# First attention of a token tower: half of the weighted values as fp16 products

## The reference

```python
def _L1_attn_ref(v, WQ, WK, WV, Wout, bout):
    q = (v @ WQ).reshape(B, S, H, C)
    k = (v @ WK).reshape(B, S, H, C)
    val = (v @ WV).reshape(B, S, H, C)
    scores = jnp.einsum('bshc,bthc->bsth', q, k) * SCALE
    A = jax.nn.softmax(scores, axis=2)
    u = jnp.einsum('bsth,bthc->bshc', A, val).reshape(B, S, H * C)
    return u @ Wout + bout
h = h + _L1_attn_ref(_layernorm(h, axis=-1), ...)
```

## Time and profile before

| what | us |
|---|---|
| time, median of 3 runs | 4917.94 (4913.84 to 4918.95) |
| the profiled execution | 4918.01 |
| its span | 4916.3 |
| first exponential of the first attention | 715.0 |
| last exponential of the first attention | 2837.2 |
| GpSimd, q to fp16 (L1473), mean of one | 0.610 |
| GpSimd, low part of q (L1475) | 1.159 |
| GpSimd, multiplication of the add (L1481) | 1.042 |
| GpSimd, addition into h (L1484) | 1.267 |
| VectorE, one row maximum (L1716) | 0.685 |
| ScalarE, one exponential (L1561) | 1.110 |

### The profile page before, as it was taken

How to read it: one execution, slowest core, us unless ns; L and a number is a source line. 1 busy time by engine, 2 the same in 40 slices (tenths; PEclk the granted TensorE clock), 3 DMA queues, 4 the chain that set the end, 5 groups by cost and what they waited for, 6 DMA issues and landing times. The chain is left out here.

```text
span 4916.3 us, 106442 instructions
## 1 busy us (share of the span) xinstructions
PE 4586.0 (93%) x42579; PEld 2033.3 (41%) x42579; DVE 3655.1 (74%) x6356; ACT 3150.1 (64%) x3450; POOL 2325.2 (47%) x2279
## 2 busy tenths in 40 slices
PE   5999969999999999999999979999999999999965
PEld 3433423333333333333333334444444444444433
DVE  4677756666666666666666678888888888888878
ACT  2444426666666666666666638888888888888844
POOL 3455553333333323233333346666666666666656
PEclk9999979999999999999999979999999999999966
DMA  4212100000000000000000000000000000000001
GB/s 102 69 52 69 35 1 1 1 1 1 1 1 1 1 1 1 1 1 1 1 1 1 1 1 2 2 2 2 2 2 2 2 2 2 2 3 2 2 7 28
DMA packets 43624, 51.44 MB, mean 10 GB/s; under 512 B 33416, under 2 KB 33544, under 8 KB 43144
## 3 DMA queue, kind: packets, MB, share of 16 engines
q1 hardware_dynamic: 40440, 44.03, 3.4%
q10 hardware_dynamic: 2704, 0.72, 0.1%
HBM read 39.73 MB, written 4.19 MB: 9 GB/s over the span
## 5 line engine op out<-in xcount | busy, mean ns | idle before, releaser
L1716 DVE TENSOR_REDUCE a_mp<-psum 128x1 f32<-128x512 f32 x2072 | 1324.8, 685 | 667.8 <-PE psum L1593 654.1
L2442 DVE TENSOR_REDUCE f_mp<-psum 128x1 f32<-128x512 f32 (+2 forms) x2352 | 1472.7, 684 | 187.1 <-PE psum L2264 171.0
L1561 ACT ACTIVATE a_prob<-psum,escale 128x1024 f32<-128x1024 f32 x1024 | 1086.3, 1110 | 524.6 <-PE psum L1642 524.6
L2224 ACT ACTIVATE f_prob<-psum,escale_f 128x1024 f32<-128x1024 f32 x1152 | 1247.2, 1112 | 217.1 <-PE psum L2341 108.4
L1650 PE MATMUL psum<-a_prob,a_v 128*64 128x512 f32 x4104 | 994.2, 605 | 0.0
L2078 POOL TENSOR_SCALAR f_hi<-f_raw,part 128x512 f16<-128x512 f32 x324 | 506.2, 1562 | 393.8 <-ACT f_raw L2182 387.5
L2264 PE MATMUL psum<-f_kf,f_qf 64*128 64x512 f16 (+2 forms) x3658 | 652.6, 307 | 40.1 <-DVE f_mp L2442 31.2
L1481 POOL TENSOR_TENSOR a_u<-a_og,a_inv 128x512 f32<-128x512 f32 x129 | 134.4, 1042 | 1167.4 <-DVE a_inv L1731 1167.4
L2354 PE MATMUL psum<-f_prob,f_vh 128*32 128x512 f32 (+3 forms) x6144 | 614.7, 495 | 9.3 <-DVE f_oc L2464 7.3
L2333 PE MATMUL psum<-f_qf,f_kf 64*128 64x512 f16 (+3 forms) x3074 | 505.5, 327 | 18.9 <-ACT f_og L2187 18.2
L1650 PEld LDWEIGHTS psum<-a_prob,a_v 128*64 128x64 f32 x4104 | 249.0, 136 | 505.1 <-issue 501.5
(11 more groups left out here) (448 smaller groups left out, 6942.4 us busy)
## 6 DMA issues: line engine op xcount, KB each, us to landing
idx<-in_itok_BS_dram SPq DMA_DIRECT2D x36, 512.0 KB, 6.0
idx<-in_itok_BS_dram SPq DMA_DIRECT2D x54, 256.0 KB, 6.9
idx<-in_x_dram SPq DMA_DIRECT2D x18, 256.0 KB, 3.6
a_qh<-a_rowT SPq DMA_DIRECT2D x258, 1.0 KB
out_dram<-h SPq DMA_DIRECT2D x16, 256.0 KB, 2.6
f_qf<-f_rowT SPq DMA_DIRECT2D x130, 4.0 KB, 1.7
wd<-in_L_ffn_Wd_dram SPq DMA_DIRECT2D x2, 256.0 KB
bd<-in_L_ffn_bd_dram ACTq DMA_DIRECT2D x16, 2.0 KB
```

The costliest lines, as they stand in the source:

```text
L1561: act.activation(prob[:, part], k.psum[:, pair:pair + 2].rearrange("p b n -> p (b n)"), ACT.Exp, scale=k.escale[:]).then_inc(s.read, 1)
L1716: dve.tensor_reduce(mp[:, tg % 2, t + 4 * r, c:c + 1], bank_of(j + r), X, ALU.max)\
L2224: act.activation(prob[:, u % NPF], k.psum[:, pair:pair + 2], ACT.Exp, scale=k.escale_f[:])\
L2442: dve.tensor_reduce(side[:, at[0]:at[-1] + 1:step], bank_of(j + r)[:, 0:len(at) * width].rearrange("p (a b) -> p a b", b=width), X, ALU.ma ...
```

## The change

Key tiles 0, 1, 4 and 5 of each head no longer go into the value sum as f32. Their exponentials are held as a high fp16 part (`ph`) and a low one (`pl`), the values too (`vh`, `vl`), and TensorE adds three fp16 products instead of one f32 product. Tiles 2, 3, 6 and 7 stay f32.

- The parts of tiles 0 and 4 are both made by GpSimd (`halve`). For tiles 1 and 5 ScalarE makes the high part (a copy behind the exponential of tile 2 or 6) and VectorE the low one (`low`).
- `A_PARTS` puts the f32 parts first: (2,3), (0,1), (6,7), (4,5), in slots 4, 6, and 1 and 2 of the next round, so the fp16 parts are used four to five steps after their exponentials.
- The copy of a head's sum moves from behind exponential 1 to behind exponential 3, and "out" from behind the third item to behind the fourth.
- GpSimd's order is written anew; its add for a head comes one round later. `twice` splits the values once per batch.
- The exponentials get a bias of 6 ln 2, a factor of 64 that the division takes out again.
- Four new tiles are cleared at the start; four semaphores of an earlier stage are used again.

```diff
-A_PARTS = ((0, 1), (2, 3), (4, 5), (6, 7))
+A_PARTS = ((2, 3), (0, 1), (6, 7), (4, 5))
+A_PART_OF = {kt: p for p, part in enumerate(A_PARTS) for kt in part}
+A_HALVED = {0: 0, 1: 1, 4: 2, 5: 3}
+A_LEVEL = 6 * math.log(2.0)
-A_VALUES_AT = (2, 4, 6, 9)
+A_VALUES_AT = (4, 6, 9, 10)
-A_EXTRA = {0: (('x', 0),), 1: (('q', 2),), 3: (('out', -1),)}
-A_COPY_AT = 1
+A_EXTRA = {0: (('x', 0),), 1: (('q', 2),), 4: (('out', -1),)}
+A_COPY_AT = 3
...
+                def twice(b, par, n):
+                    here = v[:, par, :, 0]
+                    pool.tensor_copy(vh[:, par], here).then_inc(s.p, 1)
+                    passed(pool, k.seen, s.p, n + 5)
+                    pool.tensor_tensor(vl[:, par], here, vh[:, par], ALU.subtract).then_inc(s.p, 1)
+
+                def halve(G, kt, count):
+                    at = A_HALVED[kt]
+                    passed(pool, k.seen, s.read, count)
+                    pool.tensor_copy(ph[:, at], prob[:, kt]).then_inc(s.p_high, 1)
+                    passed(pool, k.seen, s.p_high, n_half(G, kt))
+                    pool.tensor_tensor(pl[:, at], prob[:, kt], ph[:, at], ALU.subtract).then_inc(s.p_low, 1)
...
+                pool.memset(ph[:], 0.0).then_inc(s.clear, 1)
+                pool.memset(pl[:], 0.0).then_inc(s.clear, 1)
+                pool.memset(vh[:, 1], 0.0).then_inc(s.clear, 1)
+                pool.memset(vl[:, 1], 0.0).then_inc(s.clear, 1)
+                pool.memset(level[:], A_LEVEL).then_inc(s.clear, 1)
...
+                        split_q(G + 2, (x + 2) % 4, n_stream(i, x, "q", 0))
+                        halve(G, 0, n_stream(i, x, "exp", 0))
+                        if G > 1:
+                            add(i * 2 + (x - 2) // HEADS, x % 2, G)
+                        if x % HEADS == 4:
+                            prepare_batch(b, (x // HEADS + 1) % 2, b * 6)
+                        if x % HEADS == 5:
+                            split_x(b, (x // HEADS + 1) % 2, n_stream(i, x, "x", 0))
+                        halve(G, 4, n_stream(i, x, "exp", 4))
                         if x % HEADS == 3:
                             squares(i * 2 + x // HEADS)
+                        if x % HEADS == 6:
+                            twice(b, (x // HEADS + 1) % 2, b * 6)
...
-                            act.wait_ge(s.pv, n_pv(G - 1, part // 2))
+                            act.wait_ge(s.pv, n_pv(G - 1, A_PART_OF[part]))
                             act.activation(prob[:, part], k.psum[:, pair:pair + 2].rearrange("p b n -> p (b n)"),
-                                           ACT.Exp, scale=k.escale[:]).then_inc(s.read, 1)
+                                           ACT.Exp, scale=k.escale[:], bias=level[:]).then_inc(s.read, 1)
+                            if part in (2, 6):
+                                act.wait_ge(s.read, n_stream(i, x, "exp", part - 1))
+                                act.activation(ph[:, A_HALVED[part - 1]], prob[:, part - 1], ACT.Copy).then_inc(s.p_high_act, 1)
                             if part == A_COPY_AT:
                                 copy_out(G)
...
+                    if A_PARTS[p][0] in A_HALVED:
+                        pe.wait_ge(s.p_low, n_half(G, A_PARTS[p][0]))
+                        pe.wait_ge(s.p_low_dve, n_half(G, A_PARTS[p][1]))
+                        for kt in A_PARTS[p]:
+                            at = A_HALVED[kt]
+                            for a, b in ((vl, ph), (vh, pl), (vh, ph)):
+                                for half in range(2):
+                                    last = pe.matmul(ps[A_SUM][halves(half)], lhsT=a[:, bp, kt],
+                                                     rhs=b[:, at, half * HALF:(half + 1) * HALF],
...
+                def low(G, kt):
+                    at = A_HALVED[kt]
+                    dve.wait_ge(s.p_high_act, n_half(G, kt))
+                    dve.tensor_tensor(pl[:, at], prob[:, kt], ph[:, at], ALU.subtract).then_inc(s.p_low_dve, 1)
...
+                            if u == 0 and i + x:
+                                low(i * AROUND + x - 1, 5)
+                            if u == 4:
+                                low(i * AROUND + x, 1)
```

More of the change, by code:

```diff
@@ L1 @@
 from contextlib import ExitStack
+import math
 import numpy as np
@@ L704, in layer0 @@
         E = {name: k.sem("l0_" + name) for name in L_EVENTS}
+        k.spent, k.spent_at = [E[name] for name in ("gT", "eg", "wT", "gturn")], PAIRS_
         def first(pair):
@@ L1345, in attention1 @@
         prob = sb("a1_prob", [P, NPB, S], F32)
+        ph = sb("a1_ph", [P, 4, S], FP16)
+        pl = sb("a1_pl", [P, 4, S], FP16)
+        vh = sb("a1_vh", [P, 2, T, C], FP16)
+        vl = sb("a1_vl", [P, 2, T, C], FP16)
+        level = sb("a1_level", [P, 1], F32)
         un = sb("a1_un", [P, HALF], F32)
@@ L1509, in _ @@
                         G = i * AROUND + x
+                        b = i * 2 + x // HEADS + 1
+                        split_q(G + 2, (x + 2) % 4, n_stream(i, x, "q", 0))
[7 more added lines that the diff above has]
+                        halve(G, 4, n_stream(i, x, "exp", 4))
                         if x % HEADS == 3:
                             squares(i * 2 + x // HEADS)
[L1512 to L1521, removed]
+                        if x % HEADS == 6:
+                            twice(b, (x // HEADS + 1) % 2, b * 6)
+                add(NB - 1, 0, NB * HEADS)
                 add(NB - 1, 1, NB * HEADS + 1)
@@ L1643, in score, with values @@
                     return last
-                def values(x, p):
+                def values(G, x, p):
                     bp = (x // HEADS) % 2
+                    first, final = A_PARTS[0][0], A_PARTS[-1][-1]
+                    if A_PARTS[p][0] in A_HALVED:
[7 more added lines that the diff above has]
+                                                     rhs=b[:, at, half * HALF:(half + 1) * HALF],
+                                                     start=(kt == first and a is vl), stop=(kt == final and a is vh and b is ph),
+                                                     skip_group_check=True)
+                        last.then_inc(s.pv, 1)
+                        return
                     for kt in A_PARTS[p]:
@@ L1651, in values @@
                                              rhs=prob[:, kt, half * HALF:(half + 1) * HALF],
-                                             start=(kt == 0), stop=(kt == T - 1), skip_group_check=True)
+                                             start=(kt == first), stop=(kt == final), skip_group_check=True)
                     last.then_inc(s.pv, 1)
@@ L1684, in _ @@
                                             pe.wait_ge(s.read, n_stream(i, x, "exp", A_PARTS[p][-1]))
-                                            values(x, p)
+                                            values(G, x, p)
                                         if at == u + T:
                                             pe.wait_ge(s.read, n_stream(i, x - 1, "exp", A_PARTS[p][-1]))
-                                            values(x - 1, p)
+                                            values(G - 1, x - 1, p)
                                 else:
@@ L1699, in _ @@
                         pe.wait_ge(s.read, SS + SR * (NB // 2))
-                        values(-1, p)
+                        values(NB * HEADS - 1, -1, p)
                 pe.wait_ge(s.read, SS + SR * (NB // 2))
```

19 lines of the change are left out of this document (14 added, 5 removed).

## The result

The change made the kernel slower: 4998.46 us (median of 4, 4997.95 to 5001.3) against 4918.44 on the same chip, ratio 1.0165, 95% interval 1.0147 to 1.0183. That is 80 us more, where 17 were forecast; the range ended at 4985.

The account below looks back on a forecast made before the run. The prediction took TensorE to bound the kernel's first attention stretch; 4918.0 - 6 (rounds) + 13 (port) + 7.9 (start) + 1.4 (end) = 4934, stated as 4935 us, slower, range 4895 to 4985.

Parts of the forecast that it names:

- what TensorE saves: Two values parts a round as fp16, 1.39 to 1.40 against 1.87 us each; 1.05 a round with the fifth-slot wait.
- 0.86 + 1.11 + 0.06: Score of tile 7 needs exponential 5's banks, 2.03 us after tile 5's score starts; against 1.68 of work, TensorE waits 0.35.
- 1.01 + 0.95 + 1.01: ScalarE's exponential 2, copy and exponential 3 before the sums' copy, which ends at 4.43 us; TensorE waits 0.65 before "out".
- The 0.09 us wait in the fifth slot goes as well: The second row-maximum matmul's 0.09 us wait for VectorE vanishes, since "out" now stands in front of that M.
- fits: VectorE has 10.8 us of work a round and gets 2.44 more from two subtractions, for which there is room.
- The port, 13 us: VectorE and GpSimd hold each other up on a shared SBUF port pair: +13 us, bounds 0 and 18.
- The two exclude each other: At the port either VectorE comes second (0 to 13 us) or GpSimd is late (18 us), not both.
- Rival B: The port costs more: GpSimd's late subtraction delays VectorE's, the round grows 0.3 to 0.5 us, total 4970 to 5000; 11%.
- The start, 7.9: GpSimd clears four more tiles before making the first input, while TensorE stands idle: +7.9 us.
- Rival A: TensorE's saving comes through, with one or both waits on ScalarE gone: 4800 to 4890 us; 14%.
- Rival C: fp16 products are no faster in this shape, the second values part costs 1.87 us as before: 4996 us; 3%.
- The end: One more values part comes after the last exponential: +1.4 us.

Follow-up runs that it names:

- the best order: Changed kernel without bias, tile 1's copy behind exponential 4, third-slot M earlier, f32 part between scores 5 and 7, VectorE clearing, next input before GpSimd's add: 4820.48 us.
- operand: Changed kernel with the bias tile taken off the exponentials: 4980.47 us, ratio 1.0131.
- M's: Changed kernel with the third slot's row-maximum matmul pair M put ahead of the fp16 values part: 4978.06 us, ratio 1.0126.
- port: Changed kernel without VectorE's two subtractions a round, low parts of tiles 1 and 5 left zero: 4983.80 us, ratio 1.0136.

## Why the prediction was wrong

- **Sign, and what TensorE saves:** the sign of the whole was right, that of a plain round was not (16.29 forecast, 16.72 measured, 16.34 before). The price of an fp16 part was right, 1.41 to 1.42 against 1.39 to 1.40, and the best order gets 0.82 a round out of it (16.34 to 15.52), where 1.05 was put if nothing else waits.
- **The step that failed first: "0.86 + 1.11 + 0.06" and "1.01 + 0.95 + 1.01".** All use the exponential of before, 1.11. The diff adds a second 128x1 operand, and the prediction gave it no term at all. It is 0.093, in 1024 exponentials. The rows were there: a copy with no such operand 1.02, an exponential with one 1.11; the step from none to one could have been taken once more. The Trainium skill states it as well (ScalarE: Activation LUTs, "What ACT_TABLE_LOAD costs": each such operand adds about 93 ns), and the trace agrees: 1.110, 1.203. By TensorE's starts, "out" comes 4.73 after the score of tile 2 instead of 4.53 to 4.57, and tile 7 2.13 after tile 5 instead of 2.03: 0.28 of the 0.44 by which the round was missed; in time 18 us.
- **"The 0.09 us wait in the fifth slot goes as well", and VectorE "fits".** VectorE does have the time over a round. But with the f32 part gone from between them, three M's come within 2.2 us (995.38 to 997.57 above), and six reductions, 0.61 from one start to the next, take 3.7. In plain rounds this lay under ScalarE's wait; in head 2's rounds, with the means among them, it was open. The prediction gave head 2 no term; it was 20 us, with the stretches at a low clock told of below.
- **No term for starting again.** After a wait "out" takes 0.91 to the next start, not 0.84, and the M behind it 0.34, not 0.31; the f32 part to the end is as before, so 0.10 from "out" to the score of tile 5. With 0.02 to 0.03 for the fp16 parts this nearly closes the plain round: 16.29 + 0.28 + 0.10 + 0.03 = 16.70, measured 16.72 to 16.73. What it is worth in time was not run by itself.
- **The port, 13 us:** right in size (15), in part by luck, since 13 was taken between bounds of 0 and 18. About 7 us are in head 4's rounds (0.47 each, where 1.1 was put), 4 in the late head 7's, which the prediction does not name, and the rest in single long rounds. "The two exclude each other" is wrong: in the rows above VectorE comes second, and GpSimd's conversion is then held up as well. Rival B falls, though its 4970 to 5000 takes in the measured time: the plain round does not change without VectorE's subtractions.
- **The start, 7.9:** right. Two clearings on GpSimd, and TensorE's idle, 14.31 against 6.43 in the earlier trace rows:

```profile
679.90 3.52 POOL L1531 MEMSET a_ph<- 128x4096 f16 x1
683.35 3.51 POOL L1532 MEMSET a_pl<- 128x4096 f16 x1
```
```profile
692.58 1.94 PE L1675 MATMUL psum<-ident,a_v 128*128 128x128 f32 x8 [14.31 <-POOL a_v L1477]
```
- **Rival A** falls for this order: the waits are real, and removing the copy's brought 44 us. Rival C falls with the 1.41. The end cost 0.9 (4.35 of idle ahead of the last `un` against 3.46), not 1.4.

The three runs (operand, M's, port; each run's interval is some 8 us to either side) and the start add to 18 + 20 + 15 + 8 = 61 of the 80 us. The rest, some 19, no run took apart, and its cause stays open: by the table, some 8 us of it are in the plain rounds (0.39 more, of which 0.28 is the operand's) and some 8 in head 4's (15, of which 7 went with the subtractions). As waits lie over one another, the shares of single edits need not add up in any case.

## What to carry to other kernels

Price each operand that an edit adds to an instruction on the path, even one that looks free: it was 0.09 us an exponential here. A factor that cancels later might be folded into something that is computed once; no run here did that, and the best kernel leaves it out. A wait taken away shows the next one under it, so before trusting a saving look at what the removed work had kept apart, here the M's and their reductions. And read a group's duration as well as the idle ahead of it: a wait inside a group is in no list of waits.

## What the runs showed that was not expected

In four of the sixteen rounds of head 2, the granted clock of TensorE fell. Timeline of one, VectorE, GpSimd and TensorE:

```profile
1036.55 2.13 POOL L1492 TENSOR_TENSOR a_pl<-a_prob,a_ph 128x1024 f16<-128x1024 f32 x1 [0.47 <-POOL a_ph L1490]
...
1037.65 1.05 DVE L1805 TENSOR_SCALAR mean_f<-mean_f 128x8 f32<-128x8 f32 x1
...
1039.36 0.60 PE L1639 MATMUL psum<-a_xh,a_qh 64*128 64x512 f16 x1 [0.83 <-DVE a_mp L1776]
```

The f32 part behind it took 3.29 instead of 1.94. The stretch from 1039.8 to 1043.1, with the granted clock as the third number from the end:

```profile
1039.80:1043.10 3.30, 3.30 (x9) 0.77 (x8) 3.27 (x5) 0.00 (x0) 3.06 (x3) 0.57 0.02 5
```

0.57 of full speed, near the lower level of 1.2 GHz, after TensorE had waited 0.36 ahead of "out" and 0.83 ahead of the M; at 1588.7 it is 0.53 behind waits of 0.37 and 0.53. The other rounds of head 2 have like waits and kept their clock; which ones fall was not settled. Each cost 1.6 to 1.9 us; with the bias out there were six, 3.08 to 3.50 long, with the copy late seven, with both edits three, without the low parts three, and with the M moved ahead in the changed kernel none but 2.19 for the first of the stage. The rows also show VectorE's 128x8 multiplication, all in SBUF, taking 1.05 us, until GpSimd's subtraction ends at 1038.68; in the kernel before it takes 0.17. A tiny instruction waits here until a large one is done.
